# GpSimd adds up the heads of a unit ahead of weighing the heads of the unit two back, in place of the other order

## The chip, the cores and the metric

The kernel runs on one core of a Trainium2 chip. The metric is the time of one execution on the device in microseconds. TensorE (PE in the profile) does the matrix products, VectorE (DVE), ScalarE (ACT) and GpSimd (POOL) the work on single elements, and SyncE (SP) issues the transfers. Each engine works through its own instructions in order, and an instruction that waits on a semaphore holds all that stand behind it on its engine. TensorE's granted clock in the profile is a share of 2.4 GHz.

## The reference

The model has four blocks on 4 x 1024 tokens of width 128, each added to its input after a layer norm: attention within a band, a feed-forward with experts, a second attention, and the feed-forward again. The change lies in the second attention. Its softmax runs over the 16 heads (axis 1), not over the keys:

```python
def _L0_attn_b_ref(x, Wq, bq, Wk, bk, Wv, bv, Wo, bo):
    q = (x @ Wq.T + bq).reshape(B, S, H, D)          # H = 16 heads of D = 8
    ...
    scores = jnp.einsum('bqnd,bknd->bnqk', q, k) / jnp.sqrt(jnp.float32(D))
    attn = jax.nn.softmax(scores, axis=1)
    out = jnp.einsum('bnqk,bknd->bnqd', attn, v)
    out = out.transpose(0, 2, 1, 3).reshape(B, S, E)
    return out @ Wo.T + bo
```

So each pair of a query and a key needs the maximum and the sum over its 16 heads, and every query meets every key of its batch.

## The kernel before

The four blocks are four stages that follow one another. The second attention (`head_softmax_attention`, names with `head_` in the profile) runs from about 578 to 1734 us of the span. It goes through 4 batches, 8 chunks of 128 queries in each, and in a chunk 8 steps (`kt`) of 128 keys. One chunk with one step is a **unit**, and there are 256. A unit holds 16 heads x 128 keys (partitions) x 128 queries.

All loops are written out by hand, engine by engine, and the order of the calls in `chunk_of` is the order of work. A unit goes like this, where h is the half of 64 queries:

- TensorE `scores_of` (line 813) makes the scores of a half in PSUM. VectorE `largest` (line 1029) takes the negated maximum over the heads. TensorE `take_maximum` (line 835) adds it to the scores. ScalarE (line 986) writes the exponential to `ex`, a ring of 4 units (`RING`).
- GpSimd `sum_heads` adds heads 0 to 7 to heads 8 to 15 into `half` (line 770, 128 x 1024), and then two of the eight slabs to two others (line 771, 128 x 256). `half` has two buffers. It waits for both halves' exponentials and for the denominator two units back.
- Two steps later (`LAG = 2`) TensorE `denominator_of` (line 845) adds up the six slabs that are left. ScalarE `reciprocal_of` takes the logarithm (955) and the negated exponential of it twice, into `recp` in PSUM (958) and `recip` in SBUF (960).
- VectorE `weigh` (line 1036) multiplies three of every four heads with `recp`, GpSimd `weigh_rest` (line 777) the fourth (`ON_DVE = 3`: heads 3, 7, 11 and 15) with `recip`, both in place in `ex`.
- In the step after that TensorE `attend` (line 828) multiplies the 16 weighed heads with the values. It takes the heads 0, 4, 8, 12, then 1, 5, 9, 13 and so on; ahead of its first head it waits for `weigh`, and ahead of its ninth (`i == HH`) for `rest_ready`, which `weigh_rest` raises.

In step `unit` TensorE's order is: `take_maximum(unit, 0)`, `scores_of` for half 1 of this unit, `denominator_of(unit - 2)`, `scores_of` for half 0 of the next unit, `take_maximum(unit, 1)`, `attend(unit - 3)`, and in `ahead` in even steps a projection for a later chunk (kt 0, 2 and 4; those of 2 and 4 only where a next batch follows) or the output product of the chunk before (kt 6, lines 851 and 852). ScalarE's is: the exponential of half 0, the three reciprocal instructions of `unit - 2`, the exponential of half 1. The exponential of half 0 of unit + 1 waits for `attend(unit - 3)`, by the ring.

On GpSimd there is nothing in the stage but lines 770, 771 and 777; it issues no transfers there.

Of the kernel before, what the change touches and what calls it, by code (L numbers as in the profile page):

```python
# [645 lines left out]
def head_softmax_attention(nc, c, x, mv, ht, q_dram, k_dram, k_first, zero_f16, zero_f32):  # L646
# [14 lines left out]
    with Mem(nc, "head") as m:  # L661
# [98 lines left out]
        @block.gpsimd  # L760
        def _(pool):
            m.start(pool, "pool")

            def sum_heads(unit, kt):

                e, hf = ex[:, kt % RING, :, :], half[:, kt % 2, :, :]
                ch = Chain(pool, pool_chain, unit)
                pool.wait_ge(ex_ready, ONE + 2 * unit + 2)
                pool.wait_ge(den_ready, ONE + unit)
                ch.link(pool.tensor_tensor(hf, e[:, 0:8, :], e[:, 8:16, :], ALU.add))  # L770
                pool.tensor_tensor(hf[:, 0:2, :], hf[:, 0:2, :], hf[:, 2:4, :], ALU.add).then_inc(quarter_ready, 1)  # L771

            def weigh_rest(unit, kt):

                pool.wait_ge(copy_ready, ONE + unit + 1)
                e = ex[:, kt % RING, :, :].rearrange("p (g a) q -> p g a q", a=GH)[:, :, ON_DVE, :]
                pool.tensor_tensor(e, e, recip[:, kt % 2, :][:, None, :].broadcast_to([P, NG, P]),  # L777
                                   ALU.mult).then_inc(rest_ready, 1)

            def chunk_of(n, first):  # L780
                for kt in range(BT):
                    unit = n * BT + kt
                    if not (first and kt < LAG):
                        weigh_rest(unit - LAG, (kt - LAG) % BT)
                    sum_heads(unit, kt)

            chunk_of(0, True)
            for n in range(1, B * NQ):
                chunk_of(n, False)
            for kt in range(BT - LAG, BT):  # L790
                weigh_rest(LAST * BT + kt, kt)
# [891 lines left out]
```

## Time and profile before

| | us |
|---|---|
| median of 3 runs | 2047.76 |
| lowest and highest | 2047.59, 2050.64 |
| the profiled execution | 2046.14 |
| its span in the profile | 2044.3 |
| VectorE busy in the span | 1755.2 (86%) |
| ScalarE busy | 1239.2 (61%) |
| GpSimd busy | 1474.8 (72%) |
| mean granted clock of TensorE | 0.976 |

The profile is one execution. Busy shares are means over four stages of different kinds, so the second attention is read by itself: a view of busy time by stretches, the list of who waited for whom, and the timeline, which gives for each instruction its start and its length in us, the engine, the line, and what it writes and reads. Consecutive records of one line are merged into a row with their count. A line of the view by stretches gives the stretch, its length, the busy us with the count of instructions for PE, PEld, DVE, ACT and POOL in that order, the granted clock, the share of the DMA engines and the GB/s. "PEld" is the load of TensorE's weights. Matmuls overlap: the next can start before the one ahead has ended, and so a pace is read from start to start.

### The profile page before, as it was taken

What the parts mean: (1) busy time and instruction counts of PE and PEld (TensorE: products, weight loads), DVE (VectorE), ACT (ScalarE), POOL (GpSimd) and SP (SyncE); (2) the same over time, 40 slices, a digit from 0 to 9 for tenths busy, and PEclk for the clock granted to TensorE, in tenths of its full rate; (3) what the DMA queues carried; (4) which work ended last, traced back from release to release, by engine and by line L of the source; (5) the groups of instructions that cost most, each with busy time, mean ns of one, the idle gap of its engine ahead of it and who ended that gap; (6) DMA issues with size and microseconds to landing.
All of it is one profiled execution on the core that took longest, in us unless ns stands there. A gap on an engine that the chain in (4) does not pass through costs nothing. (4 is left out here: it accounts for less than half of the span.)

```text
span 2044.3 us, 55129 instructions
## 1 busy us (share of the span) xinstructions
PE 1936.5 (95%) x22048; PEld 1290.8 (63%) x22048; DVE 1755.2 (86%) x2719; ACT 1239.2 (61%) x2213; POOL 1474.8 (72%) x1046
## 2 busy tenths in 40 slices
PE   4999889999879999999999999999999998899998
PEld 2666654444357777777777777777777776544443
DVE  5777788887679999999999999999999997788876
ACT  2455456666546666666666666666666665466665
POOL 2041035656449999999999999999999998256565
PEclk9999879999979999999999999999999999799999
DMA  7322258866230000000000000000000000487672
GB/s 184 120 72 72 70 108 146 149 118 137 48 114 10 17 10 16 11 14 13 9 18 10 13 14 13 14 10 17 6 10 6 10 6 2 86 152 155 133 138 51
DMA packets 99470, 117.44 MB, mean 57 GB/s; under 512 B 31920, under 2 KB 60976, under 8 KB 98288
## 3 DMA queue, kind: packets, MB, share of 16 engines
q1 hardware_dynamic: 97920, 113.42, 25.6%
q8 instruction: 175, 2.87, 0.6%
q14 instruction: 79, 0.65, 0.1%
q10 hardware_dynamic: 1296, 0.50, 0.1%
HBM read 96.32 MB, written 17.57 MB: 56 GB/s over the span
## 5 line engine op out<-in xcount | busy, mean ns | idle before, releaser
L1029 DVE TENSOR_REDUCE head_shift<-head_score 128x64 bf16<-128x1024 f32 x512 | 624.2, 1219 | 80.2 <-PE head_score L813 68.4
L986 ACT ACTIVATE head_ex<-head_score 128x1024 f32<-128x1024 f32 x512 | 524.7, 1025 | 183.4 <-PE head_score L835 181.7
L770 POOL TENSOR_TENSOR head_half<-head_ex 128x1024 f32<-128x1024 f32 x256 | 604.0, 2359 | 40.3 <-ACT head_ex L986 40.3
L1263 POOL TENSOR_TENSOR ffn_sw<-ffn_sg,ffn_wide 128x512 f32<-128x512 f32 x256 | 324.5, 1268 | 311.5 <-ACT ffn_sg L1374 300.2
L1036 DVE TENSOR_TENSOR head_ex<-head_ex,head_recp 128x1536 f32<-128x1536 f32 x256 | 446.7, 1745 | 4.3 <-ACT head_recp L958 4.3
L845 PE MATMUL head_den<-head_half,c_ident 128*128 128x128 f32 x3072 | 385.4, 275 | 2.4 <-POOL head_half L771 2.4
L845 PEld LDWEIGHTS head_den<-head_half,c_ident 128*128 128x128 f32 x3072 | 363.4, 192 | 6.0 <-POOL head_half L771 2.6
L777 POOL TENSOR_TENSOR head_ex<-head_ex,head_recip 128x512 f32<-128x512 f32 x256 | 328.5, 1283 | 21.5 <-ACT head_recip L960 13.8
L835 PE MATMUL head_score<-head_shift,c_identb 128*128 128x512 bf16 x1024 | 309.9, 384 | 18.1 <-DVE head_shift L1029 12.0
L813 PE MATMUL head_score<-att_b_HB,att_b_GR 96*128 96x256 f16 x2048 | 311.0, 274 | 0.5 <-ACT head_ex L986 0.5
L828 PE MATMUL head_outp<-head_ex,att_b_vs 128*32 128x128 f32 x8192 | 276.5, 276 | 0.6 <-DVE head_ex L1036 0.6
L828 PEld LDWEIGHTS head_outp<-head_ex,att_b_vs 128*32 128x32 f32 x8192 | 208.1, 109 | 108.4 <-issue 107.4
L1514 DVE TENSOR_TENSOR ffn_hidden<-ffn_sw,ffn_up 128x512 f32<-128x512 f32 x256 | 178.2, 696 | 93.0 <-POOL ffn_sw L1263 86.5
L813 PEld LDWEIGHTS head_score<-att_b_HB,att_b_GR 96*128 96x128 f16 x2048 | 200.2, 98 | 80.6 <-ACT head_ex L986 3.6
L1374 ACT ACTIVATE ffn_sg<-ffn_gate 128x512 f32<-128x512 f32 x272 | 162.1, 596 | 118.7 <-PE ffn_gate L115 118.2
L1379 ACT ACTIVATE ffn_h_parts<-ffn_hidden 128x512 f16<-128x512 f32 x272 | 162.2, 596 | 94.8 <-DVE ffn_hidden L1514 88.0
L771 POOL TENSOR_TENSOR head_half<-head_half 128x256 f32<-128x256 f32 x256 | 185.6, 725 | 20.1
L955 ACT ACTIVATE head_lnd<-head_den 128x128 f32<-128x128 f32 x256 | 71.1, 278 | 208.7 <-PE head_den L845 208.7
L1522 DVE TENSOR_TENSOR ffn_h_parts<-ffn_hidden,ffn_h_parts 128x512 f16<-128x512 f32 x272 | 186.0, 684 | 0.1
L835 PEld LDWEIGHTS head_score<-head_shift,c_identb 128*128 128x128 bf16 x1024 | 72.2, 98 | 88.9 <-DVE head_shift L1029 79.4
L113 PE MATMUL ffn_down<-ffn_h_parts,c_down_parts 128*128 128x512 f16 x272 | 103.2, 379 | 3.3 <-DVE ffn_h_parts L1522 3.3
L113 PE MATMUL ffn_up<-ffn_xnT,c_up_parts 128*128 128x512 f16 x272 | 103.7, 381 | 0.9 <-DVE ffn_hidden L1514 0.7
(255 smaller groups left out, 2545.4 us busy)
## 6 DMA issues: line engine op xcount, KB each, us to landing
ffn_wide<-pair_weights SPq DMA_DIRECT2D x256, 256.0 KB, 9.7
att_b_vs<-in_zero_f SPq DMA_DIRECT2D x2, 2176.0 KB, 9.3
a_keys<-band_parts_k SPq DMA_DIRECT2D x14, 295.5 KB, 2.6
att_a_HB<-a_keys SPq DMA_DIRECT2D x56, 73.9 KB
a_queries<-band_parts_q SPq DMA_DIRECT2D x14, 271.5 KB, 3.0
att_a_GR<-a_queries SPq DMA_DIRECT2D x14, 271.5 KB
b_queries<-head_parts_q SPq DMA_DIRECT2D x32, 96.0 KB, 1.6
att_b_HB<-b_queries SPq DMA_DIRECT2D x128, 24.0 KB
```

The source lines that it names most:

```text
L113: pe.matmul(out, w[:, i, 0, :], hi, start=start, stop=False)
L770: ch.link(pool.tensor_tensor(hf, e[:, 0:8, :], e[:, 8:16, :], ALU.add))
L777: pool.tensor_tensor(e, e, recip[:, kt % 2, :][:, None, :].broadcast_to([P, NG, P]), ALU.mult).then_inc(rest_ready, 1)
L813: last = pe.matmul(score[:, h, g // 2, (g % 2) * GH * QS:(g % 2 + 1) * GH * QS].rearrange("p (a w) -> p a w", a=GH), GR[:, buf, g, kt * P: ...
L828: last = pe.matmul(outp[g * 32:(g + 1) * 32, 0:P], vs[:, buf * BT + kt, at:at + 32], ex[:, kt % RING, n, :], start=(kt == 0 and n4 == 0), ...
L835: last = pe.matmul(score[:, h, k, :].rearrange("p (a w) -> p a w", a=NH // 2), c["identb"][:, :], shift[:, h, :][:, None, :].broadcast_to( ...
L845: last = pe.matmul(den[:, 0:P], c["ident"][:, :], half[:, kt % 2, k, :], start=(i == 0), stop=(i == len(SLABS) - 1))
L986: act.activation(ex[:, kt % RING, :, h * QS:(h + 1) * QS], score[:, h, :, :].rearrange("p k (a w) -> p (k a) w", a=NH // 2), ACT.Exp, scal ...
L1029: dve.tensor_reduce(shift[:, h, :], score[:, h, :, :].rearrange("p k (a w) -> p w k a", a=NH // 2), AX.XY, ALU.max, negate=True).then_inc( ...
L1036: dve.tensor_tensor(e, e, recp[:, 0:P][:, None, None, :].broadcast_to([P, NG, ON_DVE, P]), ALU.mult).then_inc(prob_ready, 1)
L1263: pool.tensor_tensor(sw[:, unit % 2, :], sg[:, unit % 2, :], wide[:, k % 2, i, :], ALU.mult).then_inc(sw_ready, 1)
L1522: dve.tensor_tensor(h_parts[:, unit % LAG, 1, :], hidden[:, unit % 2, :], h_parts[:, unit % LAG, 0, :], ALU.subtract).then_inc(low_ready, 1)
```

## The change

In GpSimd's `chunk_of` the call of `sum_heads` moves ahead of that of `weigh_rest`. Operands, semaphores and the other engines' code stay as they are.

```diff
             def chunk_of(n, first):
                 for kt in range(BT):
                     unit = n * BT + kt
+                    sum_heads(unit, kt)
                     if not (first and kt < LAG):
                         weigh_rest(unit - LAG, (kt - LAG) % BT)
-                    sum_heads(unit, kt)
```

The stage's start on GpSimd shows best which unit a row belongs to. L770 and L771 are the sums of a unit, L777 is the weighing; `head_copy_ready` comes from line 960, `head_ex_ready` from line 986. Before:

```order
L770 TENSOR_TENSOR head_half<-head_ex 128x1024 [waits head_den_ready,head_ex_ready]
L771 TENSOR_TENSOR head_half<-head_half 128x256 [waits head_pool_chain]
L770 TENSOR_TENSOR head_half<-head_ex 128x1024 [waits head_den_ready,head_ex_ready]
L771 TENSOR_TENSOR head_half<-head_half 128x256 [waits head_pool_chain]
L777 TENSOR_TENSOR head_ex<-head_ex,head_recip 128x4x128 [waits head_copy_ready]
L770 TENSOR_TENSOR head_half<-head_ex 128x1024 [waits head_den_ready,head_ex_ready]
```

And with the change, the same place:

```order
L770 TENSOR_TENSOR head_half<-head_ex 128x1024 [waits head_den_ready,head_ex_ready]
L771 TENSOR_TENSOR head_half<-head_half 128x256 [waits head_pool_chain]
L770 TENSOR_TENSOR head_half<-head_ex 128x1024 [waits head_den_ready,head_ex_ready]
L771 TENSOR_TENSOR head_half<-head_half 128x256 [waits head_pool_chain]
L770 TENSOR_TENSOR head_half<-head_ex 128x1024 [waits head_den_ready,head_ex_ready]
L771 TENSOR_TENSOR head_half<-head_half 128x256 [waits head_pool_chain]
L777 TENSOR_TENSOR head_ex<-head_ex,head_recip 128x4x128 [waits head_copy_ready]
```

Before, the weighing of unit 0 stood behind the sums of unit 1; now it stands behind those of unit 2, and so on through all units: each weighing has moved past one pair of sums. At the stage's end on GpSimd, before:

```order
L777 TENSOR_TENSOR head_ex<-head_ex,head_recip 128x4x128 [waits head_copy_ready]
L770 TENSOR_TENSOR head_half<-head_ex 128x1024 [waits head_den_ready,head_ex_ready]
L771 TENSOR_TENSOR head_half<-head_half 128x256 [waits head_pool_chain]
L777 TENSOR_TENSOR head_ex<-head_ex,head_recip 128x4x128 [waits head_copy_ready] x2
```

With the change:

```order
L777 TENSOR_TENSOR head_ex<-head_ex,head_recip 128x4x128 [waits head_copy_ready]
L770 TENSOR_TENSOR head_half<-head_ex 128x1024 [waits head_den_ready,head_ex_ready]
L771 TENSOR_TENSOR head_half<-head_half 128x256 [waits head_pool_chain]
L777 TENSOR_TENSOR head_ex<-head_ex,head_recip 128x4x128 [waits head_copy_ready] x3
```

Three weighings stand behind the last sums instead of two. TensorE's row is the same before and after; this is where it waits for the weighing, in a step with an output product:

```order
L835 MATMUL head_score<-head_shift,c_identb 128x512 [waits head_shift_ready]
L835 MATMUL head_score<-head_shift,c_identb 128x512
L828 MATMUL head_outp<-head_ex,att_b_vs 32x128 [waits head_prob_ready]
L828 MATMUL head_outp<-head_ex,att_b_vs 32x128 x7
L828 MATMUL head_outp<-head_ex,att_b_vs 32x128 [waits head_rest_ready]
L828 MATMUL head_outp<-head_ex,att_b_vs 32x128 x7
L851 MATMUL head_proj<-c_b_bo,c_ident 128x128 [waits head_outT_ready,head_v_done]
```

Nothing has moved there: the wait for `head_rest_ready` is at the ninth head, behind eight heads that need VectorE's part alone.

## Rows read from the trace of the kernel before

**Rows 1.** The page: busy us, share and count of each engine

```profile
PE 1936.5 (95%) x22048; PEld 1290.8 (63%) x22048; DVE 1755.2 (86%) x2719; ACT 1239.2 (61%) x2213; POOL 1474.8 (72%) x1046
```

**Rows 2.** Busy us by stretch, head stage; then clock, DMA share, GB/s

```profile
920.00:1020.00 100.00, 98.45 (x1284) 73.92 (x1287) 92.69 (x84) 65.40 (x121) 95.71 (x69) 1.00 0.04 12
...
sum 1100.00, PE 1084.83 PEld 815.11 DVE 1026.53 ACT 722.90 POOL 1061.03; mean PE 98.62 PEld 74.10 DVE 93.32 ACT 65.72 POOL 96.46
```

**Rows 3.** Waits, 591 to 1735 us: total us, times, longest

```profile
POOL head_ex L777 <- ACT head_recip L960: 13.8, 32, 1.4
...
PE head_den L845 <- POOL head_half L771: 2.4, 1, 2.4
```

**Rows 4.** Timeline, TensorE: start us, length us of later `attend` calls

```profile
1042.08 1.08 PE L828 MATMUL head_outp<-head_ex,att_b_vs 128*32 128x128 f32 x32
...
1542.22 1.08 PE L828 MATMUL head_outp<-head_ex,att_b_vs 128*32 128x128 f32 x32
...
1577.32 1.08 PE L828 MATMUL head_outp<-head_ex,att_b_vs 128*32 128x128 f32 x32
```

**Rows 5.** Timeline, 1005 to 1017 us: TensorE, ScalarE, GpSimd

```profile
1005.65 0.60 PE L835 MATMUL head_score<-head_shift,c_identb 128*128 128x512 bf16 x2
...
1006.19 1.08 PE L828 MATMUL head_outp<-head_ex,att_b_vs 128*32 128x128 f32 x32
...
1006.26 1.29 POOL L777 TENSOR_TENSOR head_ex<-head_ex,head_recip 128x512 f32<-128x512 f32 x1
...
1006.29 1.03 ACT L986 ACTIVATE head_ex<-head_score 128x1024 f32<-128x1024 f32 x1 [0.28 <-PE head_score L835]
...
1007.51 2.36 POOL L770 TENSOR_TENSOR head_half<-head_ex 128x1024 f32<-128x1024 f32 x1
...
1007.75 0.59 PE L835 MATMUL head_score<-head_shift,c_identb 128*128 128x512 bf16 x2
...
1008.62 1.50 PE L845 MATMUL head_den<-head_half,c_ident 128*128 128x128 f32 x12
...
1010.40 0.60 PE L835 MATMUL head_score<-head_shift,c_identb 128*128 128x512 bf16 x2
...
1010.74 0.29 ACT L960 ACTIVATE head_recip<-head_lnd 128x128 f32<-128x128 f32 x1
...
1010.92 1.08 PE L828 MATMUL head_outp<-head_ex,att_b_vs 128*32 128x128 f32 x32
...
1011.11 1.28 POOL L777 TENSOR_TENSOR head_ex<-head_ex,head_recip 128x512 f32<-128x512 f32 x1 [0.44 <-ACT head_recip L960]
...
1011.94 0.61 PE L835 MATMUL head_score<-head_shift,c_identb 128*128 128x512 bf16 x2
...
1012.35 2.37 POOL L770 TENSOR_TENSOR head_half<-head_ex 128x1024 f32<-128x1024 f32 x1
...
1015.41 1.08 PE L828 MATMUL head_outp<-head_ex,att_b_vs 128*32 128x128 f32 x32
...
1015.48 1.29 POOL L777 TENSOR_TENSOR head_ex<-head_ex,head_recip 128x512 f32<-128x512 f32 x1
...
1016.60 0.59 PE L835 MATMUL head_score<-head_shift,c_identb 128*128 128x512 bf16 x2
```

**Rows 6.** Timeline cut at 1569.23 us: the records of one `attend` so far

```profile
1568.84 0.64 PE L828 MATMUL head_outp<-head_ex,att_b_vs 128*32 128x128 f32 x16
```

**Rows 7.** Timeline of the head stage's end, GpSimd and TensorE

```profile
1726.11 0.73 POOL L771 TENSOR_TENSOR head_half<-head_half 128x256 f32<-128x256 f32 x1
...
1726.89 1.60 PE L845 MATMUL head_den<-head_half,c_ident 128*128 128x128 f32 x12 [2.42 <-POOL head_half L771]
...
1731.02 1.08 PE L828 MATMUL head_outp<-head_ex,att_b_vs 128*32 128x128 f32 x32 [0.64 <-DVE head_ex L1036]
```

**Rows 8.** All of `denominator_of` (min/median/max ns); timeline, the stage's start

```profile
L845 PE MATMUL head_den<-head_half,c_ident x3072: 273/275/417, 591.9 to 1728.2; 128*128 128x128 f32 x192
...
581.20 1.01 PE L835 MATMUL head_score<-head_shift,c_identb 128*128 128x512 bf16 x2 [1.78 <-DVE head_shift L1029]
```

## The prediction

> **What bounds the kernel now.** Read the page's busy lines first: TensorE is busy for 95% of the span, the most of any engine [rows 1]. The change touches one stage only, the second attention ("head"), so the next view is the busy time in stretches of 100 us inside it: TensorE 98.6 us, GpSimd 96.5, VectorE 93.3 (mean of eleven stretches), at a granted clock of 1.00 in the one shown [rows 2]. Three engines are nearly full, so neither share says what bounds; the waits do. In the whole stage GpSimd waited 13.8 us in 32 units for ScalarE's reciprocal, and TensorE waited for GpSimd once, 2.4 us, at the very end [rows 3]. GpSimd delays nobody in the steady state; it follows. What sets the pace is TensorE's own row of work: from one weighted sum `attend` to the same one a chunk of eight units later it takes 1042.08 - 1006.19 = 35.89 us, 4.486 us per unit, in the first three batches, and 1577.32 - 1542.22 = 35.10 us, 4.3875 us per unit, in the last [rows 4, 5], where the projections for a next batch fall away. GpSimd's own work per unit is 3.13 us from the start of the head sums to the start of the weighing (1012.35 to 1015.48) and 1.25 us from there to the next sums (1006.26 to 1007.51) [rows 5], 4.38 us: below TensorE's pace in the first batches, level with it in the last.
>
> **What the change moves.** It adds and removes no instruction. The weighing of unit u-2 (line 777), which stood ahead of the head sums of unit u, now stands behind them. Two things follow.
>
> The head sums come earlier by up to 1.25 us. They are read by `denominator_of` two steps later, and TensorE doesn't wait for them now [rows 3], so this is worth nothing. GpSimd's waits for the reciprocal vanish too; GpSimd bounds nobody, so they are worth nothing either, except under the first rival.
>
> The weighing comes later, and behind it stand a wait and 3.13 us of work that it did not have in front of it: the sums of unit u need the second exponential of unit u, and a GpSimd instruction that waits holds all behind it. Who waits for the weighing? `attend(u-2)`, in step u+1 on TensorE, takes three quarters of its heads from VectorE and the last, heads 3, 7, 11 and 15, from GpSimd; the code makes it wait for line 777 at its ninth head. Take the step whose `take_maximum(u, 1)` starts at 1005.65 [rows 5]. Today the weighing of u-2 starts at 1006.26 and ends at 1007.55; `attend(u-2)` starts at 1010.92 and comes to its ninth head 0.40 us later (16 of its 32 records, two per head, have started within 0.39 us [rows 6]), at 1011.32. It has 3.8 us to spare. With the change: the second exponential starts at 1006.29 and ends at 1007.32; GpSimd starts 0.08 us after what it waits for (ScalarE's 1010.74 + 0.29 = 1011.03, GpSimd at 1011.11), so the sums start at 1007.40, the weighing at 1010.53, and it ends 1.29 us later at 1011.82. TensorE takes up GpSimd's result 0.05 us after its end (1726.11 + 0.73 = 1726.84, TensorE at 1726.89 [rows 7]), at 1011.87: **0.55 us late**. For the next step the same working gives 1012.06 (end of the exponential), 1012.14, 1015.27, 1016.56 and 1016.61, against 1015.41 + 0.40 = 1015.81: 0.80 us late. TensorE is the engine with nothing to spare, so the cover is gone at the first unit.
>
> **What a late unit costs in the long run.** The delay isn't added up unit by unit, because a stalled TensorE also delays the next exponential. The path closes on itself every two units, and its length is the price. From `take_maximum(u, 1)`:
> - to the second exponential, 1005.65 to 1006.29: 0.64
> - the exponential: 1.03; to the sums: 0.08
> - start of the sums to start of the weighing: 3.13; the weighing: 1.29
> - to TensorE: 0.05
> - from the ninth head to the next `take_maximum`: 1010.92 to 1011.94 is 1.02, less the first eight heads' 0.40: 0.62
> - from there to `take_maximum(u+2, 1)`, 1007.75 to 1010.40, through the scores, the denominator and the scores: 2.65
>
> The sum is 9.49 us for two units [rows 5 to 7]. In the loops whose `attend` stands in an even step, that step's extra work lies in it as well: a projection costs 1015.41 to 1016.60 less 1.02, 0.17 us, the output product 1006.19 to 1007.75 less 1.02, 0.54 us [rows 5]. Per chunk that is three projections and an output product in four loops, 0.26 us each. The other loops have none of it, but TensorE works in order and the longer kind sets the pace: (9.49 + 0.26) / 2 = **4.875 us per unit** against 4.486. In the last batch two projections fall away, (0.17 + 0.54) / 4 = 0.18, and (9.49 + 0.18) / 2 = 4.835 against 4.3875. Both are above every engine's own work, so this path, and not an engine, becomes the bound. The sum: 192 units x 0.389 = 74.7 us and 64 x 0.4475 = 28.6 us, **+103 us**. Against the profiled execution's own 2046.14 us that is 2149; against the median, 1.6 us above it, 2151. Outside the stage nothing changes.
>
> **Bounds of what the trace doesn't show.** No row shows TensorE released in the middle of `attend`. Below: a hand-over that costs nothing, a weighing that counts with its 1.25 us to the next start, and a ninth head halfway through (0.51 us to go) take 0.20 us from the loop, 26 us over 256 units. Above: after its wait at 1726.89 TensorE took 1.60 us for twelve matmuls [rows 7] instead of 1.50 (1008.62 [rows 5]); 0.1 to 0.15 us more per loop, up to 20 us. I take the middle since 0.05 us is the very hand-over from GpSimd to TensorE. If the two kinds of loop did not tie, and only 9.49 / 2 = 4.745 held, the cost would be 192 x 0.259 + 64 x 0.3575 = 73 us, 2121.
>
> Whether the weighing costs its waiter 1.29 us, its duration, or 1.25 [rows 5] can't be seen in GpSimd's own row, where the next instruction starts a little before the end. The Trainium skill ("GPSIMD Engine Reference", section "Instruction dispatch") says that completion holds up only what waits on the instruction's semaphore, not GpSimd's next instruction. By that rule the full duration counts, as taken; with 1.25 the sum would be some 5 us less.
>
> **Rivals.** (1) GpSimd is the bound after all, and the time falls. For it: 96 to 98% busy [rows 2], a period in the last batch equal to its own work, and waits for the reciprocal that the new order removes. Then the stage would run at 4.38 us per unit; it takes 1136 us from its first to its last denominator [rows 8], so 1121 us, 15 us less: 2033. It needs the weighing to reach `attend` in time, which decides it: more than 0.55 us must be found in a path of which every piece is a row. (2) No change: TensorE reaches the ninth head later than worked out, by those 0.55 to 0.8 us, since the profile's pipelined matmuls are modelled: 2048. (3) The late half tips TensorE's clock. TensorE will stand still some 0.5 us per unit. Against it: after waits of 2.42 and 0.64 us at the stage's end, `attend` still takes its usual 1.08 us, the length at 2.4 GHz [rows 7]. Were it to fall to 1.2 GHz, a pair of matmuls of line 835 took 1.01 us at the stage's start (581.20) against 0.60 [rows 5, 8]; a unit grows by about 2.5 us, and each tenth of the stage spent there costs 64 us more: 2215 and above. The Trainium skill ("TensorE: Matmul & The Clock Gate", section "What's actually happening") says that the clock is lowered after idleness and restored by activity; the rows at the end speak against that happening here. (4) That the order isn't changed at all is excluded by GpSimd's instruction rows.
>
> **How the numbers follow.** The loop: 0.86, 2151. Rival 1: 0.05. Rival 2: 0.05. Rival 3: 0.04. The range of 8 in 10 is the loop's with its bounds, and stretched to the untied case less a third of the lower bound: 2112 to 2172. About 0.2% (4 us) is what a measurement tells from no change; faster 0.05, same 0.05, slower 0.90.
>
> **What the profile after would show.** Right: TensorE waits at line 828 for GpSimd's `head_ex` (line 777) in most units, some 0.4 us per unit and 100 us in all; GpSimd waits at line 770 for ScalarE's exponential, about 0.5 us per unit, and no longer at line 777; the sums start 0.08 us behind each second exponential; chunks of eight are 39.0 us apart in the first batches and 38.6 in the last; TensorE's busy share in the stage falls to about 90%, its clock stays at 1.00; all other stages keep their length. Wrong: a TensorE that waits only in every other unit (the untied case), no wait at line 828 (rivals 1 and 2), or a granted clock below 1.00 inside the stage.

## The result

| | us |
|---|---|
| before, median of 4 runs | 2049.2 |
| changed, median of 4 runs (2138.5 to 2144.1) | 2142.7 |
| ratio, 95% interval | 1.0451 [1.0437, 1.0465] |
| profiled execution of the changed kernel; its span | 2142.58; 2140.7 |

The new order costs 92 us by the ratio and 93.5 by the two medians, 4.5%. The forecast was 2151 us, 103 us more than before, in a range of 2112 to 2172.

The page of the changed kernel, in the form of [rows 1], and of its list of groups the lines 770, 828 and 777 (busy us, mean ns, and behind the bar the idle time before them with its releaser):

```profile
PE 1977.5 (92%) x22048; PEld 1283.0 (60%) x22048; DVE 1765.2 (82%) x2719; ACT 1238.2 (58%) x2213; POOL 1478.3 (69%) x1046
...
L770 POOL TENSOR_TENSOR head_half<-head_ex 128x1024 f32<-128x1024 f32 x256 | 604.8, 2363 | 151.3 <-ACT head_ex L986 140.9
...
L828 PE MATMUL head_outp<-head_ex,att_b_vs 128*32 128x128 f32 x8192 | 319.8, 279 | 65.8 <-POOL head_ex L777 63.6
...
L777 POOL TENSOR_TENSOR head_ex<-head_ex,head_recip 128x512 f32<-128x512 f32 x256 | 325.3, 1271 | 0.3 <-ACT head_recip L960 0.3
```

The instructions are the same and take no longer than before: line 770 takes 2363 ns on average against 2359, VectorE's weighing (1036) 1744 against 1745. What has grown is waiting, in two places that answer to [rows 3]. Some of it is hidden in TensorE's busy time, 41 us more than before, to which the last section comes back. The waits in the head stage, 591 to 1830 us (total us, times, longest):

```profile
PEld head_outp L828 <- POOL head_ex L777: 121.0, 220, 1.0
...
POOL head_half L770 <- ACT head_ex L986: 101.9, 157, 1.6
PE head_outp L828 <- POOL head_ex L777: 63.6, 128, 0.7
...
POOL head_ex L777 <- ACT head_recip L960: 0.3, 1, 0.3
```

GpSimd's wait for the reciprocal is gone but for 0.3 us, where [rows 3] had 13.8. In its place line 770 waits for the exponential, and TensorE, which waited for nobody on GpSimd in the steady state, waits at line 828 for the weighing. The busy time by stretches, as [rows 2]:

```profile
920.00:1020.00 100.00, 94.51 (x1193) 68.17 (x1190) 87.35 (x79) 60.38 (x109) 88.75 (x62) 1.00 0.04 10
...
sum 1195.00, PE 1125.27 PEld 807.90 DVE 1039.56 ACT 723.75 POOL 1068.51; mean PE 93.77 PEld 67.32 DVE 86.63 ACT 60.31 POOL 89.04
```

The last of these twelve stretches is only 95 us long, so the means of the last line are low; per 100 us, TensorE falls from 98.6 to 94.2 and GpSimd from 96.5 to 89.4. The clock stays at 1.00 from 620 to 1815 us. At the stage's very end it doesn't: behind a wait of 1.92 us ahead of the last denominator it falls to 0.50, which is 1.2 GHz (a stretch, then the timeline), and the last three `attend` (96 records) take 4.38 us in one row:

```profile
1824.00:1826.00 2.00, 2.00 (x48) 1.80 (x44) 1.81 (x2) 0.39 (x2) 1.49 (x2) 0.50 0.03 8
...
1821.81 1.66 PE L845 MATMUL head_den<-head_half,c_ident 128*128 128x128 f32 x12 [1.92 <-POOL head_half L771]
1823.40 4.38 PE L828 MATMUL head_outp<-head_ex,att_b_vs 128*32 128x128 f32 x96
```

From the start of the last denominator's final matmul to the output product it is 5.1 us here (1823.14 to 1828.28) and 4.4 before, so this costs under 1 us. The stage's length, from the first to the last denominator, as [rows 8]:

```profile
L845 PE MATMUL head_den<-head_half,c_ident x3072: 273/275/422, 593.6 to 1823.1; 128*128 128x128 f32 x192
```

That is 1229.5 us against 1136.3 before: 93.2 of the 96.4 us by which the two spans differ lie inside the stage.

The path itself can be read off the timeline of the changed kernel (start us, length us; TensorE, ScalarE and GpSimd), in the form of [rows 5]:

```profile
996.36 0.60 PE L835 MATMUL head_score<-head_shift,c_identb 128*128 128x512 bf16 x2
...
1001.22 1.27 POOL L777 TENSOR_TENSOR head_ex<-head_ex,head_recip 128x512 f32<-128x512 f32 x1
...
1001.37 0.65 PE L828 MATMUL head_outp<-head_ex,att_b_vs 128*32 128x128 f32 x16
1002.54 0.65 PE L828 MATMUL head_outp<-head_ex,att_b_vs 128*32 128x128 f32 x16 [0.53 <-POOL head_ex L777]
...
1005.71 1.27 POOL L777 TENSOR_TENSOR head_ex<-head_ex,head_recip 128x512 f32<-128x512 f32 x1
...
1006.32 0.60 PE L835 MATMUL head_score<-head_shift,c_identb 128*128 128x512 bf16 x2
1006.84 1.08 PE L828 MATMUL head_outp<-head_ex,att_b_vs 128*32 128x128 f32 x32
...
1006.95 1.02 ACT L986 ACTIVATE head_ex<-head_score 128x1024 f32<-128x1024 f32 x1
...
1008.05 2.36 POOL L770 TENSOR_TENSOR head_half<-head_ex 128x1024 f32<-128x1024 f32 x1 [1.07 <-ACT head_ex L986]
...
1010.08 0.60 PE L813 MATMUL head_score<-att_b_HB,att_b_GR 96*128 96x256 f16 x4
1010.79 0.60 PE L835 MATMUL head_score<-head_shift,c_identb 128*128 128x512 bf16 x2
...
1011.17 1.27 POOL L777 TENSOR_TENSOR head_ex<-head_ex,head_recip 128x512 f32<-128x512 f32 x1
...
1011.33 0.64 PE L828 MATMUL head_outp<-head_ex,att_b_vs 128*32 128x128 f32 x16
1012.50 0.64 PE L828 MATMUL head_outp<-head_ex,att_b_vs 128*32 128x128 f32 x16 [0.53 <-POOL head_ex L777]
1013.07 0.23 PE L113 MATMUL head_proj<-att_b_xnT,c_b_parts 128*128 128x128 f16 x1
...
1013.25 0.59 PE L835 MATMUL head_score<-head_shift,c_identb 128*128 128x512 bf16 x2
...
1015.90 0.60 PE L835 MATMUL head_score<-head_shift,c_identb 128*128 128x512 bf16 x2
```

A late `attend` first. The weighing at 1001.22 ends at 1002.49. Eight heads of `attend` have gone from 1001.37 on, and the ninth was due 0.40 us later, at 1001.77; the other eight start only at 1002.54, and the row of 32 records has broken into two of 16. TensorE has lost 0.77 us, of which the view lists 0.53 as idle. In the next step the weighing at 1005.71 is over at 1006.98, `attend` starts at 1006.84, and the release comes in time: its row has the usual 1.08 us. In the step after it is late again (1011.33, 1012.50).

These three steps have the one in-time release of their chunk. Over the whole stage the ninth head starts 0.05 to 0.06 us after the weighing's end, and so is held by it, in 221 of 256 units: in 127 of them the row has lost 0.55 to 0.98 us, in the other 94 some 0.1 to 0.4. The list of TensorE's waits shows only the first kind (128), the list of its weight loads both (220). And the sums start 0.08 us after the end of the second exponential in 254 of 256 units.

Now the path from one `take_maximum(u, 1)` to the next but one: TensorE at 1006.32, ScalarE's exponential at 1006.95 and over at 1007.97, the sums at 1008.05, the weighing at 1011.17 and over at 1012.44, the ninth head at 1012.50, the projection at 1013.07, `take_maximum(u+2, 0)` at 1013.25 and `take_maximum(u+2, 1)` at 1015.90. That is 9.58 us with a projection. The path ahead of it, over an output product, goes from 996.36 to 1006.32, 9.96 us. The starts of `attend` are 5.04 to 5.48 us apart over the even steps and 4.48 to 4.55 over the odd ones; a chunk of eight takes 38.72 us, 4.84 per unit, where [rows 4, 5] had 35.89.

The sum closes over the stage too. From the first to the last record of a call, the 256 calls of `attend` take 109 us more than before. Part of this was spent before in another wait, the one for VectorE's maximum: `take_maximum(u, 1)`, which can start 0.44 us after the scores ahead of it, comes 34 us late in total before and 20 us in the changed kernel. The difference, 95 us, agrees with the 93.2.

### The profile page after: what moved, and what is told of

Same layout as the page of the kernel before. It is cut to its first block and busy times, and to the rows that moved or that the text cites. A ratio compares the mean times of both kernels' runs of the same rounds, so it can differ in the third digit from the quotient of the medians.

```text
span 2140.7 us, 55129 instructions
## 1 busy us (share of the span) xinstructions
PE 1977.5 (92%) x22048; PEld 1283.0 (60%) x22048; DVE 1765.2 (82%) x2719; ACT 1238.2 (58%) x2213; POOL 1478.3 (69%) x1046
## 5 line engine op out<-in xcount | busy, mean ns | idle before, releaser
L770 POOL TENSOR_TENSOR head_half<-head_ex 128x1024 f32<-128x1024 f32 x256 | 604.8, 2363 | 151.3 <-ACT head_ex L986 140.9
L1036 DVE TENSOR_TENSOR head_ex<-head_ex,head_recp 128x1536 f32<-128x1536 f32 x256 | 446.6, 1744 | 3.9 <-ACT head_recp L958 3.9
L828 PE MATMUL head_outp<-head_ex,att_b_vs 128*32 128x128 f32 x8192 | 319.8, 279 | 65.8 <-POOL head_ex L777 63.6
L828 PEld LDWEIGHTS head_outp<-head_ex,att_b_vs 128*32 128x32 f32 x8192 | 195.8, 109 | 229.1 <-POOL head_ex L777 121.0
L777 POOL TENSOR_TENSOR head_ex<-head_ex,head_recip 128x512 f32<-128x512 f32 x256 | 325.3, 1271 | 0.3 <-ACT head_recip L960 0.3
L771 POOL TENSOR_TENSOR head_half<-head_half 128x256 f32<-128x256 f32 x256 | 185.4, 724 | 20.1
```

The costliest lines, as they stand in the source:

```text
L828: last = pe.matmul(outp[g * 32:(g + 1) * 32, 0:P], vs[:, buf * BT + kt, at:at + 32], ex[:, kt % RING, n, :], start=(kt == 0 and n4 == 0), ...
L1036: dve.tensor_tensor(e, e, recp[:, 0:P][:, None, None, :].broadcast_to([P, NG, ON_DVE, P]), ALU.mult).then_inc(prob_ready, 1)
```

## The experiments

`take_maximum(u, 1)` to `take_maximum(u+2, 1)`, through the second exponential, the sums, the weighing and the second half of `attend`, is called the path below; it takes 9.68 us per two units on average over a chunk. Two rivals stood against it. Rival A: GpSimd's own row, which now begins each unit with a wait for the exponential, is the bound, and TensorE's wait only shows it. Rival B: the new overlap of GpSimd's work with that of other engines slows one of them. All ratios are against the kernel before on the same chip, where it had a median of 2047.8 to 2049.1 us.

### Less behind the release: the thirteenth head

GpSimd weighs heads 3, 7, 11 and 15, and `attend` takes these as its thirteenth to sixteenth. The wait stands at the ninth.

```diff
                 for i in range(NH):
                     n4, g = divmod(i, NG)
-                    if i == HH:
+                    if i == NH - NG:
                         pe.wait_ge(rest_ready, ONE + unit + 2)
```

> The changed order, with the wait for GpSimd's weighing in attend moved from the ninth head to the thirteenth, the first that GpSimd has weighed. Nothing else moves. Theory (the path of two units through the second half of attend): four heads, 8 records of 0.025 us, 0.20 us, leave the path: from 9.68 us per two units to 9.48, 0.10 us per unit, 25 us in all: before plus 68 us, about 2117. Chunks 37.9 us apart in place of 38.7. Rival A (GpSimd is the bound, by its own work and its waits for the exponential in its own row): TensorE's wait is a symptom, no change, before plus 93. Rival B (the new overlap slows an engine, by contention): no change either.

Measured: 2114.4 us, ratio 1.0325 [1.0309, 1.0340], 67 us more than before and, by the ratios, 26 less than the changed kernel. A chunk takes 37.87 us. TensorE's wait at line 828 has shrunk by the same kind of amount (total us, times, longest; 63.6 in the changed kernel):

```profile
PE head_outp L828 <- POOL head_ex L777: 37.0, 126, 0.5
```

Both rivals forecast no change. An edit that touches nothing but which head waits gives the 0.20 us per two units that the path says.

### More behind the release: the first head, in both orders

```diff
-                    if i == HH:
+                    if i == 0:
                         pe.wait_ge(rest_ready, ONE + unit + 2)
```

> The changed order, with attend's wait for GpSimd's weighing at its first head in place of the ninth. Theory: the first eight heads, 0.40 us, come to stand behind the release, so the path grows from 9.68 to 10.08 us per two units, 0.2 us per unit, 51 us in all: before plus 144, about 2193; chunks about 40.3 us apart. A theory in which the wait at line 828 is a symptom of another bound gives 2142, no change.

Measured: 2207.9 us, ratio 1.0781 [1.0765, 1.0797], 160 us more than before; a chunk takes 40.80 us. The direction is the theory's, and the size is 16 us above it. The timeline of this kernel, GpSimd and TensorE (its view cut at 1015 us), shows where from:

```profile
1000.63 1.26 POOL L777 TENSOR_TENSOR head_ex<-head_ex,head_recip 128x512 f32<-128x512 f32 x1
...
1002.04 1.08 PE L828 MATMUL head_outp<-head_ex,att_b_vs 128*32 128x128 f32 x32 [1.13 <-POOL head_ex L777]
...
1003.05 0.23 PE L113 MATMUL head_proj<-att_b_xnT,c_b_parts 128*128 128x128 f16 x1
```

The weighing ends at 1001.89, and TensorE starts at 1002.04, 0.15 us later, where a release in the middle of `attend` took 0.05 (1002.49 to 1002.54 above); and the eight heads that now stand behind the release take 0.43 us, where 0.40 had been put: 1.01 for the whole call (1002.04 to 1003.05), less 0.57 to 0.58 for the half behind the ninth head. Together 0.53 us per two units, 68 us over the stage; the measured step from the changed kernel is 65 us by the medians and 68 by the ratios. The wait itself, total us, times and longest:

```profile
PE head_outp L828 <- POOL head_ex L777: 151.7, 146, 1.4
```

On the order of before the same edit is the control.

> The same edit on the order of before, as a control. Theory: the weighing has 3.8 us to spare at the ninth head and 3.4 at the first: no change, within 3 us of before. If the place of the wait had a price of its own, it would show here.

Measured: 2049.0 us, ratio 1.0004 [0.9995, 1.0014]. There the place of the wait has no price, since the weighing is over 3.4 us ahead of it.

### The wait without the work: weighing first, but not before the exponential

```diff
                 pool.wait_ge(copy_ready, ONE + unit + 1)
+                pool.wait_ge(ex_ready, ONE + 2 * min(unit + LAG, LAST * BT + BT - 1) + 2)
```

> The order of before, weighing first, but the weighing also waits for the second exponential of the unit whose sums follow it: the wait of the new order without the 3.13 us of sums ahead of the weighing. Theory: the path is 9.68 less 3.1, 6.6 us per two units, 3.3 per unit, far below 4.486: within 4 us of before. Rival A (a GpSimd row that begins with a wait for the exponential is what costs): GpSimd idles as in the changed kernel, and the time is near 2142. Rival B: the overlap is nearly that of before, no change.

Measured: 2050.4 us, ratio 1.0007 [0.9998, 1.0017]. The chunks take 35.89 us, as before. GpSimd does wait for the exponential ahead of the weighing (line 778 here), as far as its row leaves room for it:

```profile
POOL head_ex L778 <- ACT head_ex L987: 10.4, 31, 0.9
```

So the new wait at the head of GpSimd's row is not what costs. Rival A in the form "a row that begins with that wait" is out; the 3.1 us of sums between the wait and the weighing are needed.

### Less work ahead of the weighing: between the two sums

```diff
             def sum_heads(unit, kt):
                 ...
-                ch.link(pool.tensor_tensor(hf, e[:, 0:8, :], e[:, 8:16, :], ALU.add))
+                pool.tensor_tensor(hf, e[:, 0:8, :], e[:, 8:16, :], ALU.add).then_inc(pool_chain, 1)
+
+            def sum_quarters(unit, kt):
+
+                hf = half[:, kt % 2, :, :]
+                pool.wait_ge(pool_chain, ONE + unit + 1)
                 pool.tensor_tensor(hf[:, 0:2, :], hf[:, 0:2, :], hf[:, 2:4, :], ALU.add).then_inc(quarter_ready, 1)
...
+                    sum_heads(unit, kt)
                     if not (first and kt < LAG):
                         weigh_rest(unit - LAG, (kt - LAG) % BT)
-                    sum_heads(unit, kt)
+                    sum_quarters(unit, kt)
```

> GpSimd adds heads (line 770) of this unit, weighs the unit two back, and then adds the quarters (line 771). The weighing starts 2.3 us after the exponential instead of 3.1. Theory: the path loses 0.8 us: 9.68 less 0.8 is 8.88 per two units, 4.44 per unit, just below the 4.486 of before: within 5 us of before, about 2050. Rival A: GpSimd's row still begins with the wait for the exponential and holds the same work: most of the 93 us stays, 2120 or above. Rival B: the weighing overlaps other work than in both kernels; nothing can be said, but a full return to the time of before would be a chance.

Measured: 2052.8 us, ratio 1.0024 [1.0015, 1.0033], some 5 us more than before. GpSimd's timeline: the large sum (769), the weighing (781) 2.32 us behind it in place of 3.13, the small sum (775):

```profile
1002.97 2.37 POOL L769 TENSOR_TENSOR head_half<-head_ex 128x1024 f32<-128x1024 f32 x1
1005.29 1.27 POOL L781 TENSOR_TENSOR head_ex<-head_ex,head_recip 128x512 f32<-128x512 f32 x1
1006.51 0.75 POOL L775 TENSOR_TENSOR head_half<-head_half 128x256 f32<-128x256 f32 x1
```

The first three batches keep the 35.89 us of before to the hundredth. In the last batch a chunk takes 35.4 to 35.5 us where it took 35.10, some 3 of the 5 us. The expectation had compared the path with the pace of the first batches alone. There the path (9.41 + 0.18 - 0.81 = 8.78 us per two units, 4.39 each) and the 4.39 of before are level, so a step in which the path is the longer shows, and TensorE's weight loads wait 22 times for the weighing (line 833), 20 of them in the last batch. The other 2 us are not placed; the interval alone leaves 3 to 7 us for the whole difference.

Those waits, and GpSimd's for the exponential:

```profile
POOL head_half L769 <- ACT head_ex L991: 41.2, 141, 0.8
...
PEld head_outp L833 <- POOL head_ex L781: 4.7, 22, 0.3
```

### Later use: `attend` one step on

`LAG, RING = 2, 8` in place of `2, 4`; `attend(unit - 4)` in place of `attend(unit - 3)` with the conditions on `kt` moved by one, `copy_out` likewise; and `xn`, of use only ahead of the units, laid into the ring's last slot.

```diff
-    LAG, RING = 2, 4
+    LAG, RING = 2, 8
...
-                        attend(unit - (LAG + 1), n - 1 if back else n, (kt - LAG - 1) % BT, 1 - buf if start and back else buf)
+                        attend(unit - (LAG + 2), n - 1 if back else n, (kt - LAG - 2) % BT, 1 - buf if start and back else buf)
...
-                        if h == 0 and kt == LAG + 1 and not first:
+                        if h == 0 and kt == LAG + 2 and not first:
                             copy_out(n - 1)
```

> The changed order, with attend one step later (the unit four back in place of three back), a ring of 8 units of exponentials in place of 4, and xn laid into the ring's last slot to make room. The same work on every engine. Theory: the same path closes after three units in place of two: 9.7 / 3 = 3.2 us per unit, no longer the bound: within 5 us of before, 2050. Rival A: GpSimd's row is untouched, 2142. Rival B: GpSimd's overlap with VectorE is untouched, 2142.

Measured: 2048.7 us, ratio 1.0004 [0.9994, 1.0013], with chunks of 35.89 us. GpSimd has the changed order word for word, and the 92 us are gone. Its wait for the exponential is left in 26 places, and one of them, the stage's first, makes up 38.9 of the 49.5 us:

```profile
POOL head_half L770 <- ACT head_ex L986: 49.5, 26, 38.9
```

This settles both rivals: GpSimd's row is that of the changed kernel, and the weighing has a step longer until it is read. The deeper ring came along with it and wasn't run alone. In the changed kernel the ring held nobody up, though: all listed waits of line 986 are for `take_maximum` (269.6 us, 331 times), which on TensorE stands behind the `attend` that the ring waits for.

### What bounded the kernel before, and whether the cost adds to it

The kernel before had a second path: in its steps of 4.5 us without extra work TensorE's weight loads wait for VectorE's maximum. The row stands in the same list as [rows 3]:

```profile
PEld head_score L835 <- DVE head_shift L1029: 77.0, 264, 0.9
```

VectorE's small work of a step stood behind its weighing and so ahead of the next step's first maximum. Here it stands between the two maxima:

```diff
                     largest(2 * unit + 1, 1)
+                    ahead(b, q, kt)
                     if not (last and kt == BT - 1):
                         largest(2 * unit + 2, 0)
                     if not (first and kt < LAG):
                         weigh(unit - LAG, (kt - LAG) % BT)
-                    ahead(b, q, kt)
```

and in `ahead` the low parts of queries and keys move from kt 1 and 3 to kt 2 and 4.

> The order of before on GpSimd; on VectorE the small work of a step (ahead) stands between its two maxima, where it stood behind the weighing, and two pieces of it (the low parts of queries and keys) one step later. The next step's first maximum then starts right behind the weighing. Theory of the kernel before: TensorE's steps of 4.5 us without extra work contain a wait of some 0.25 us for that maximum; they shrink to 4.3, a chunk from 35.9 to 35.0 us: 22 us less than before, about 2026. If TensorE's own row were the whole bound, no change.

Measured, on the order of before: 2024.7 us, ratio 0.9889 [0.9874, 0.9903]. That is 23 us below the kernel before, and level with the two fastest of the kernels below. A chunk takes 34.98 us. TensorE's work is the same, so its own row was not the whole bound before. The stretch that [rows 2] shows, in this kernel:

```profile
920.00:1020.00 100.00, 100.00 (x1323) 75.86 (x1322) 95.12 (x88) 66.56 (x122) 98.11 (x70) 1.00 0.05 13
```

TensorE's row shows no gap any more, which doesn't mean that it never waits. The weight loads' wait has shrunk and not gone:

```profile
PEld head_score L835 <- DVE head_shift L1029: 54.9, 271, 1.2
```

And with the changed order:

> The same move on VectorE together with the changed order on GpSimd. Theory: the path through the second exponential, the sums, the weighing and the second half of attend doesn't contain VectorE's small work, so it stays at 9.68 us per two units and the 22 us are not to be had: before plus 93, 2142. If the changed order costs a fixed amount on top of whatever bounds the kernel, it would be 22 us less, 2120.

Measured: 2141.3 us, ratio 1.0460 [1.0443, 1.0478], the time of the changed kernel. A chunk takes 38.73 us, in steps of 4.29 and 5.31 us: what VectorE gives back in one step TensorE waits away in the next, 90.3 us at line 828 in place of 63.6:

```profile
PE head_outp L828 <- POOL head_ex L777: 90.3, 128, 0.9
```

The order's cost is no fixed amount: it is the difference between the path and whatever else would bound the stage, 92 us here and 117 us against the faster version.

### The changed order with both cures

> The changed order on GpSimd with both cures: attend a step later with a ring of 8 (as e4) and VectorE's small work between its maxima (as e7). Theory: the path closes over three steps, 3.2 us per unit, and so costs nothing even at the faster pace of e7: within 4 us of e7, some 22 us less than before, 2026. If the new order had a cost of its own beside that path, it would show now that TensorE's waits for VectorE are gone: 2035 or more.

Measured: 2027.5 us, ratio 0.9893 [0.9876, 0.9909], chunks of 34.98 us: with `attend` a step later the new order is as good as the old also at the faster pace.

> As e9, with the weighing between the two sums of GpSimd (as e2), which hides the 0.08 us that line 771 waits for line 770: GpSimd's row is 4.30 us per unit in place of 4.38. If GpSimd's row has become the bound in e7 and e9 (98% busy, 34.98 us per chunk of eight, 4.372 each), a few us more are to be had, up to 0.08 x 256 = 20 us where nothing else comes late; TensorE's own row (4.20 us and the extra work, 34.7 us per chunk) allows at most 0.03 us per unit, 8 us in all: 2018 to 2026.

Measured: 2026.1 us, ratio 0.9890 [0.9871, 0.9908], chunks again of 34.98 us. The 0.08 us per unit on GpSimd are worth nothing, so GpSimd's 98% is not the bound there either. TensorE's row has 100 us busy in 100 (stretch of this kernel):

```profile
920.00:1020.00 100.00, 100.00 (x1323) 76.30 (x1321) 94.75 (x87) 67.08 (x122) 97.86 (x69) 1.00 0.05 13
```

Even so it is not the whole bound. Its own pieces add up to 4.20 us per step (4.37 less the projection's 0.17), three projections and an output product, 34.65 us per chunk in the first batches. The 0.33 that are left show in the four steps of a chunk without extra work, which take 4.29. In the timeline of this kernel (818 the scores, 840 `take_maximum`) the second pair of rows belongs to such a step, from the `attend` at 1001.75 to the one at 1006.04. The last row is from the list of waits:

```profile
1000.79 0.60 PE L818 MATMUL head_score<-att_b_HB,att_b_GR 96*128 96x256 f16 x4
1001.23 0.60 PE L840 MATMUL head_score<-head_shift,c_identb 128*128 128x512 bf16 x2
...
1004.99 0.60 PE L818 MATMUL head_score<-att_b_HB,att_b_GR 96*128 96x256 f16 x4
1005.50 0.60 PE L840 MATMUL head_score<-head_shift,c_identb 128*128 128x512 bf16 x2
...
PEld head_score L840 <- DVE head_shift L1034: 56.3, 274, 1.2
```

`take_maximum(u, 1)` starts 0.44 us after the scores in the step ahead of it and 0.51 in this one, 0.07 to 0.08 later, and the last row names VectorE's maximum as what the weight loads wait for. That this is the rest of the bound is read from the trace; no run tests it.

## Why the prediction was right

- **Who follows whom.** GpSimd was busy for 96% and bounded nobody, read from the waits and not from the shares. The control on the old order and the wait alone leave the time as it was, as a follower would.
- **What set the pace before** was read wrongly in part: "TensorE's own row of work". Its weight loads waited 264 times for VectorE's maximum, 77.0 us, a row that the prediction didn't look at, and moving VectorE's small work alone took 23 us away. It did no harm to the forecast, because the sum subtracts the pace as measured and the new path is longer than it with or without these waits.
- **The sums' head start and the vanished wait for the reciprocal were put at nothing.** GpSimd's 13.8 us of waits went to 0.3 and brought nothing.
- **The lateness.** 0.55 and 0.80 us were worked out for the first pass. In the steady state of the changed kernel the `attend` at 1001.37 loses 0.77 us (due 1001.77, released 1002.54).
- **The path over two units.** The mechanism held; its length was put at 9.49 us and the extra work. The timeline of after gives 9.96 over the output product and 9.58 over a projection, less 0.54 and 0.17 of extra work: 9.42 and 9.41. The larger part of the miss is the term "from the ninth head to the next `take_maximum`", 0.62: released in the middle, TensorE needs 0.57 (1012.50 to 1013.07). The weighing took 1.27 us and not 1.29, the exponential 1.02 and not 1.03. Per unit that is 4.84 against 4.875, 7 us over the first three batches; in the last batch 38.4 us per chunk against 8 x 4.835 = 38.7 (the prediction's list of signs says 38.6) take 2 to 3 us more. That is the distance from +103 to +93. The upper bound, 0.1 to 0.15 us more per loop after a wait, had no ground in its row: in the kernel before the twelve matmuls of line 845 take 1.60 us at 1722.86 too, with no wait listed ahead of them.
- **The Trainium skill's rule on completion** ("GPSIMD Engine Reference", section "Instruction dispatch"), that it holds up what waits on the instruction's semaphore and not GpSimd's next instruction. Here TensorE goes on 0.05 us after the weighing's full duration (1001.22 + 1.27 = 1002.49, TensorE at 1002.54). The trace agrees with the rule, though the two counts lie only some 0.03 us apart.
- **The signs.** The sums do start 0.08 us behind the second exponential, in 254 of 256 units, and the ninth head is held by the weighing in most units, 221 of 256. Wrong was the picture of an even 0.4 us: the loss alternates, some 0.75 us in one unit and some 0.2 in the next, and the list of TensorE's waits has only the large ones (128 times, 0.5 us each). So "waits only in every other unit", set down as the sign of the untied case at 73 us, appeared in that list at the full cost. The longer loop sets the pace. The shorter one, whose `attend` has no extra work behind it, has 0.26 us less of its own, and this goes into the wait for VectorE's maximum: `take_maximum` starts 0.71 us after the scores (1010.08 to 1010.79) in place of 0.44. TensorE's busy share, put at 90%, was 94.2%, because part of the standing still counts as busy: line 828 has 319.8 us in place of 276.5 for the same matmuls.
- **Rivals.** The first two did not happen. Of the third, a little did, and not where it was looked for. With half a microsecond or more of standing still in every other unit the granted clock was 1.00 in every stretch from 620 to 1815 us. But at the stage's end it fell to 0.50, behind a wait of 1.92 us, where the prediction had taken the same place in the kernel before (2.42 and 0.64 us of waits, `attend` at its usual 1.08) as a sign that it would not. Luck had a part there; the price was under 1 us.

## What to carry to other kernels

An engine that is 96% busy may still be a follower with microseconds to spare: ask who waits for it. Here its results had 3.8 us to spare, and the swap cost time because it made one of them late. So, for a swap on such an engine, take the trace, shift the moved instruction by what is put ahead of it, waits included, and compare with the start of its reader. If it is late, don't add the lateness up: find the path by which the reader gets back to the moved instruction, divide its length by the number of units it spans, and compare with the present pace; one more unit of distance (a deeper ring, a later reader) removed the whole cost here. And look for the other waits at the present pace: TensorE's 98.6 us busy in 100 hid a wait for VectorE that was worth 23 us.

## What the runs showed of the hardware

A run of small matmuls that waited in its middle goes on 0.05 us after GpSimd's instruction ends (1002.49, 1002.54; 0.05 to 0.06 in 221 units of the changed kernel). One released at its first matmul, in the kernel with the wait at the first head, starts 0.15 us after (1001.89, 1002.04; 0.14 to 0.15 in 224 units). Of a stall in the middle of such a run, some is listed as busy time: the busy time of line 828 grew by 43 us with the same 8192 matmuls (276.5 to 319.8), and the list has 64 us of waits beside it. Idle time alone would have missed 40% of what TensorE lost there. The lists of the weight loads showed more of these waits than the list of the matmuls, in this stall and in the one for VectorE's maximum.
